# The sums of squares of one RMS norm on ScalarE instead of VectorE's statistics, in a four-layer kernel on one core

## The reference

```python
def _rmsnorm(x, w):
    n = xf * jax.lax.rsqrt(jnp.mean(xf * xf, axis=-1, keepdims=True) + EPS)
    return n.astype(x.dtype) * w
...
h = x + _gqa(_rmsnorm(x, attn_norm_w), wq, wk, wv, wo)
out = h + _moe(_rmsnorm(h, ffn_norm_w), gate_w, expert_w)
```

## Time and profile before

| what | value |
|---|---|
| three timed runs | 1502.51, 1512.09, 1514.85 us; median 1512.09 |
| the profiled execution | 1492.19 us, span of its instructions 1490.4 us |
| mean granted clock of TensorE | 0.902 |
| TensorE busy | 1239.1 us, 83% |
| VectorE busy | 1028.9 us, 69% |
| ScalarE busy | 838.9 us, 56% |
| GpSimd busy | 773.5 us, 52% |

### The profile page before, as it was taken

One profiled execution on the slowest core, in us unless ns is written; L12 is line 12 of the kernel. 1 busy time (PEld: TensorE's weight loads), 2 busy tenths in 40 slices (PEclk: granted clock), 3 DMA queues, 4 the chain that ended last, 5 costly groups with the idle time before them and its releaser, 6 DMA issues.

```text
span 1490.4 us, 39703 instructions
## 1 busy us (share of the span) xinstructions
PE 1239.1 (83%) x15796; PEld 959.4 (64%) x15797; DVE 1028.9 (69%) x2439; ACT 838.9 (56%) x2675; POOL 773.5 (52%) x793
## 2 busy tenths in 40 slices
PE   5878879878978888887898888778887578998997
PEld 4667667664756666666677656666665156776776
DVE  4467787886877687868568789886653856655562
ACT  3697676546459558657837645563543455434431
POOL 4048497486287419631762783781101767545442
PEclk8697888998989899999789899998998589999999
DMA  6000000000000000000000000001001000000000
GB/s 165 5 2 1 1 2 1 2 2 1 22 1 2 21 2 1 2 23 1 1 21 2 2 1 2 17 10 47 1 12 48 20 2 3 10 10 9 16 10 15
DMA packets 26703, 19.20 MB, mean 13 GB/s; under 512 B 6521, under 2 KB 24217, under 8 KB 26393
## 3 DMA queue, kind: packets, MB, share of 16 engines
q1 hardware_dynamic: 24936, 15.78, 3.7%
q10 hardware_dynamic: 1584, 0.89, 0.2%
HBM read 12.73 MB, written 3.93 MB: 11 GB/s over the span
## 4 chain that ended last, share of the span: by engine, by line
PE 25%; DVE 11%; ACT 6%; POOL 4%; issue 4%; POOLq 0%; ACTq 0%; DVEq 0%
PE bank L1164 4%; ACT arena L1219 2%; PE pair L1138 2%; DVE arena L1631 2%; PE bank L1207 2%; PE bank L1197 2%; PE bank L525 1%; PE bank L878 1%; PE pair L1111 1%; PE pair L495 1%; PE bank L530 1%; PE pair L853 1%; PE pair L826 1%; ACT arena L1266 1%; DVE arena L1635 1%
## 5 line engine op out<-in xcount | busy, mean ns | idle before, releaser
L1219 ACT ACTIVATE arena<-bank 128x512 f32<-128x512 f32 (+5 forms) x363 | 187.0, 545 | 253.9 <-PE bank L530 83.2
L1631 DVE TENSOR_REDUCE arena<-pair 128x8 f32<-128x1024 f32 (+2 forms) x224 | 240.3, 1095 | 101.2 <-PE pair L580 41.5
L2317 POOL TENSOR_TENSOR arena<-arena 128x512 f32<-128x512 f32 x160 | 184.6, 1153 | 65.7 <-DVE arena L1751 58.9
L1266 ACT ACTIVATE arena<-pair,arena 77x128 f32<-77x128 f32 x512 | 178.1, 369 | 27.4 <-DVE arena L1631 20.2
L2322 POOL TENSOR_TENSOR arena<-arena 128x512 f32<-128x512 f32 x128 | 182.5, 1426 | 10.0
L2255 POOL TENSOR_SCALAR arena<-arena 128x4 f32<-128x4 f32 x64 | 20.3, 317 | 266.4 <-DVE arena L1638 213.1
L2338 POOL TENSOR_TENSOR arena<-arena 128x512 f32<-128x512 f32 x64 | 67.2, 1065 | 147.4 <-ACT arena L1219 110.1
L525 PE MATMUL bank<-ident 128*128 128x128 f32 x780 | 126.5, 303 | 10.9 <-POOL subscale L2208 4.3
L525 PEld LDWEIGHTS bank<-ident 128*128 128x128 f32 x780 | 110.6, 211 | 29.3 <-issue 12.4
L2262 POOL TENSOR_SCALAR_AFFINE_SELECT arena<-arena 77x1024 f32<-77x1024 f32 x64 | 69.3, 1095 | 108.6 <-ACT arena L1603 108.2
L1603 ACT ACTIVATE arena<-pair 77x1024 f32<-77x1024 f32 x64 | 63.1, 1016 | 103.3 <-PE pair L1138 95.9
(11 more groups left out here) (304 smaller groups left out, 2990.3 us busy)
## 6 DMA issues: line engine op xcount, KB each, us to landing
arena<-in_ctx_turned SPq DMA_DIRECT2D x16, 154.0 KB, 2.6
arena<-in_x SPq DMA_DIRECT2D x8, 256.0 KB, 4.3
out<-arena SPq DMA_DIRECT2D x8, 256.0 KB, 2.5
spill<-arena SPq DMA_DIRECT2D x7, 256.0 KB, 2.0
arena<-spill SPq DMA_DIRECT2D x7, 256.0 KB, 5.1
arena<-in_ctx SPq DMA_DIRECT2D x8, 154.0 KB
arena<-in_ctx_turned SPq DMA_DIRECT2D x1, 1232.0 KB, 7.0
wexp<-in_L_ffn_expert_w SPq DMA_DIRECT2D x1, 512.0 KB, 4.2
```

The costliest lines, as they stand in the source:

```text
L1219: return act.activation(dst, src, func, bias=bias, scale=scale)
L1266: ins = act.activation(e0[0:CTX, (2 * SEQS * g + u) % 3, tokens(i)], o.bank[0:CTX, tokens(i)], ACT.Exp, bias=negmax0[0:CTX, u, i:i + 1], a ...
L1631: return dve.tensor_reduce(dst, src, X, op, **kw)
L2317: pool.tensor_tensor(into, xvs[:, b, ex * SHD:(ex + 1) * SHD].unsqueeze(1).broadcast_to([128, SH, SHD]), gates[g % 2][:, b, 0:SH, ex].unsq ...
```

## The change

The statistics of h and the two small products leave VectorE. ScalarE gets a new step at the start of its `m1`: four activations with the function Square, each over one sequence's 128 channels, whose accumulator gives the sum of squares. Their elementwise output goes to `nm`, which GpSimd overwrites later. The division by 128 is put into GpSimd's `rsqrt`. ScalarE's order string gets eight letters n, one a group; the other engines' strings and the fillers stay. The new step stands, in ScalarE's order, right behind: the copy of `ysT` of group 2 (group 0), of layer 1's `nT1` of group 2 (group 1), the second copy `eF` of a sequence of group 4 (group 2), layer 1's `aT1` of group 4 (group 3), the copy of `ysT` of group 6 (group 4), layer 2's last copy of group 4 (group 5), `aT1` of group 7 (group 6) and layer 2's last copy of group 6 (group 7).

```diff
@@ ORDER["A", "scalar"]: eight letters n added, the rest of the string is the same
@@ ScalarE
             def m1(g):
                 yield
+                o = E["f1", g, "o"]
+                act.wait_ge(o.drained, o.n + 1)
+                if g:
+                    act.wait_ge(m_x, g)
+                    act.wait_ge(lnm.n, g)
+                for b in range(SEQS):
+                    ins = act.activation(nm[:, b, :], hres[g % 2][:, b, :], ACT.Square, accum_out=lnm.mv[:, b, 1:2])
+                ins.then_inc(C.give(lnm.var), 1)
+                yield
                 o = E["m", g, "n"]
@@ VectorE
                 o = E["f1", g, "o"]
                 dve.wait_ge(o.drained, o.n + 1)
-                stats(lnm, h).then_inc(C.give(dve_step), 1)
-                dve.wait_ge(dve_step, C.last(dve_step))
-                tt(msq, lnm.mv[:, :, 0], lnm.mv[:, :, 0], ALU.mult).then_inc(C.give(dve_step), 1)
-                dve.wait_ge(dve_step, C.last(dve_step))
-                tt(lnm.mv[:, :, 1], lnm.mv[:, :, 1], msq, ALU.add).then_inc(C.give(lnm.var), 1)
                 tt(x, x, h, ALU.add)
@@ GpSimd
-            def rsqrt(dst, src, eps):
-                pool.tensor_scalar(dst, src, eps, None, ALU.add).then_inc(C.give(pool_step), 1)
+            def rsqrt(dst, src, eps, each=1.0):
+                if each == 1.0:
+                    pool.tensor_scalar(dst, src, eps, None, ALU.add).then_inc(C.give(pool_step), 1)
+                else:
+                    pool.tensor_scalar(dst, src, each, eps, ALU.mult, ALU.add).then_inc(C.give(pool_step), 1)
...
-            def spread(ln, eps):
+            def spread(ln, eps, each=1.0):
                 pool.wait_ge(ln.var, C.next(ln.var))
-                return rsqrt(ln.rstd, ln.mv[:, :, 1], eps)
+                return rsqrt(ln.rstd, ln.mv[:, :, 1], eps, each)
...
-                spread(lnm, RMS_EPS).then_inc(C.give(pool_step), 1)
+                spread(lnm, RMS_EPS, 1.0 / CH).then_inc(C.give(pool_step), 1)
```

More of the change, by code:

```diff
@@ L56 @@
         "wawwwaiabwbwwwwwwwbbbbbbcccaacabdbddbddebebdcfecfebfbfecefbfaaegfceafhffbbgfbbcfhbdcbgdddbdceheaabde"
[L57 to L62, removed]
+        "fgecffeafehfbfbgibfeecihfbgifbifcibffhibjcgjbdjjhcdglldddhedellfleleffiififleelgefifiehnfgfnfnfjnfjn"
+        "njhjnngnndnhdnldldnnllnglldnhnilldeeaeainefanibffbignennneinnihfbfnfnjcjbgjnjnbeechfnbfnfbgncfbnifhn"
+        "fcaagladldhddlldililbleelifeedibfiefnfecnbfnfjejnfegjnfnjfbnhnfgcbnnnfnfhbbgnllnchnbgcnillnhalaldail"
+        "liddiddbeibinebcnffdenjjfnebjnbncfejnnbefnfnbgnnefecffnbhnfcngnfnfillhadagaldlbdhddbebgebdchefcellff"
+        "bibibfiefegcefibfhecillfgjjffjjhnfdfngnldlndndndnnhdelelnnngnllnfenellnfefffhfnigennnnefeifnfinhninn"
+        "gififnnfhnngjnjjnjnhngllinhlliilylyilyyyyylyyyiyinyyynyjjynjjnnnnnllnnnllnnllnnllnnnnnnnnnnnnnnnnnnn",
     ("B", "scalar"):
```

## The result

The changed kernel is slower: the ratio to the kernel before on record is 1.0097, 95% interval 1.0067 to 1.0126, which is 14.6 us, where 8 were forecast. That ratio leaves out the executions of the kernel before that were more than 1.5% above its fastest, 9 of 20, and none of the changed kernel's, so it lies high. Over all 20 and 20 executions the medians are 1502.76 and 1512.87 us, 10.1 us apart, and the means 1502.9 and 1511.1 us: 8.2 us or 0.54%, 95% interval 3.5 to 12.9 us. A second measurement gave a ratio of 1.0106 (1.0065 to 1.0147), and 7.5 us between the means.

The account below looks back on a forecast made before the run. It named no single bound: in stage A four hand-ordered engines make each other late. Lateness of 9.7 us less VectorE's 1.68 gave +8.0 us on 1512.09, so 1520 us; 8 in 10 for 1502 to 1532.

Parts of the forecast that it names:

- small loss: Whole kernel: late norm in groups 1 to 6 outweighs VectorE's gain, +8 us, 1514 to 1526 us; chance 0.50.
- What is removed: VectorE, second norm's statistics: 1.68 us a group goes, 13.4 us in eight groups.
- What is added: ScalarE: four Square and accumulator-read pairs a group, 1.45 us, bounds 1.2 and 2.4; 11.6 us in all.
- lower bound that L1298's row gave: ScalarE's squares: by a 336 ns SBUF-to-SBUF activation a pair may cost some 0.30 us, 1.2 us for four.
- When the squares start: ScalarE's fixed order: never waits for `hres` but comes late, so normalised activations come 14.5 us later together.
- What is late next: Waits behind the squares and norm on TensorE, VectorE and GpSimd, group by group: 9.7 us of lateness paid.
- The sum: Stage A: 9.7 us of lateness less VectorE's 1.68 us credited once in group 0, leaving +8.0 us.
- VectorE as the bound: Stage A: VectorE's 13.4 us come off and ScalarE's lateness is absorbed, 1499 us; chance 0.11.
- Table loads: ScalarE: Square needs two table loads a group, 16 x 1.28 = 20.5 us, giving 1541 us; chance 0.05.
- Absorbed both ways: TensorE's idle stretches and fillers take it up; lateness and gain cancel, 1512 us; chance 0.22.
- All of GpSimd's lateness: Every wait for the norm counts: 14.5 us instead of 9.7, no VectorE gain, 1527 us; chance 0.12.
- Against which time: Base of the forecast: 8 us put on the 1512.09 us median of three timed runs, giving 1520 us.

Follow-up runs that it names:

- run without statistics: Kernel before with VectorE's statistics and two products removed and nothing in their place, GpSimd's root made of a constant; ratio 0.9989.
- relay without statistics: Kernel before, VectorE's statistics removed; GpSimd waits for a small ScalarE copy of a constant mean square at the change's place; ratio 1.0006.

## Why the prediction was right, and by how much it was off

It forecast a small loss from lateness in groups 1 to 6, and a small loss from lateness it is. The size came out near, 8.2 us between the means for 8.0, but in part by luck: the terms of the sum came to some 3 us less than forecast, and a part of the loss goes with TensorE's clock, which the sum had no term for. By its steps:

- *What is removed.* The block is gone and worth 13.4 us of VectorE time, as the sum had it. That the time hardly gains by it was right too (0.9989).
- *What is added.* 1.27 to 1.29 us for four pairs, not 1.45; the value lay near the lower bound that L1298's row gave. The squares take 302 ns on average, where the exponentials' first took 370. GpSimd's two-operation instruction stands at 0.19 us everywhere, where the addition took 0.5 to 0.6 beside VectorE.
- *When the squares start.* Right in all eight groups: ScalarE never waited for `hres`, and each block begins where the activation ahead ends. The root came later, against the end of `hres`, by 2.2, 2.6, 1.9, 0.9, 3.5, 1.2 and -0.4 us in groups 1 to 7, where 2.55, 2.83, 2.88, 1.17, 3.71, 1.51 and -0.16 were forecast: 11.9 us for 14.5. The shorter square is 1.2 us of the difference, and 0.7 more lies in group 3, where the second profile of the change has 2.6 us. The root and the scaling got 0.4 us shorter besides, so the norm's end is 9.1 us late in all.
- *What is late next.* Every wait named is in the trace, group 1's for ScalarE (0.83 to 1.06 us), group 3's for ScalarE (1.94 to 3.10), group 2's and 5's for GpSimd. How much later each place named comes against `hres`, as the mean of two profiles before and two after, groups 1 to 6: 0.8, 2.2, 1.2, -0.1, 3.1 and 0.3 us, where the sum had 1.45, 2.83, 1.45, 0.5, 2.7 and 0.9. In group 2 two profiles of one kernel differ by some 1.5 us. In group 5 VectorE's copy of the gate came 12.65 us after `hres` instead of 9.52. In group 7 the norm is 0.8 us sooner, where 0.16 was forecast.
- *The sum.* With these sizes it gives 6.7 us instead of 9.7, and 5.0 with VectorE's 1.68 set off once. At equal clock the change costs 4.1 and 5.3 us: so far the adding was sound. The rest, up to 8.2 and 7.5 us, goes with a mean clock of 0.886 and 0.890, where the kernel before had 0.892. The trace shows a way to it, half clock behind the new waits; how much of the rest is that and how much is the scatter of the clock isn't shown. Against the ratio's 14.6 us the sum is short by nearly half.
- *The rivals.* VectorE as the bound is ruled out by the run without statistics. Table loads: three, as before. Absorbed both ways is what the run with earlier squares shows, not the change. All of GpSimd's lateness (1527 us and more) isn't reached.
- *Against which time.* The median of three, 1512.09, was high: with 20 runs it is 1502.76. So the predicted 1520 us is 7 above the 1512.87 found: 9.3 us too much in the time before, and 2.1 too little in the change. The time found even lies in the stretch given to *absorbed both ways* (1507 to 1514) and not in that of the small loss (1514 to 1526); it is the comparison with the kernel before that shows the loss. The range of 1502 to 1532 holds the time in either case.

What stays open is how far lateness itself brings the clock down. The kernels with a late norm and VectorE's block in place have the lowest mean clock (0.884, twice) and those in which the squares are in time the highest (0.896, 0.898), which speaks for it. The kernel with the squares done twice speaks against a plain rule: its norm is the latest and its mean clock is 0.890, as in the change's second series. Single profiles can't decide it: both profiles of before are of short executions, those without statistics and of the relay without statistics (1514.20 us) are of long ones, and the part before the first changed instruction alone shifts by up to 12 us.

## What to carry to other kernels

When work moves to another engine with a fixed order, compare two clocks for each repetition: when its input is ready, and when the engine's queue comes to it. Moving the squares one to four steps up in ScalarE's order took 1.1% down to 0.2% by the ratios, 9.2 us over all executions, with no other edit; the sizes of the two blocks (1.27 us against 1.68) didn't decide it. Time saved on an engine that isn't late is worth little, here 13.4 us of VectorE for 0.1%. And where the executions of one kernel spread by 2%, an effect of 0.5% is read from the means over all of them, with the granted clock beside, and not from two profiles.

## What the runs showed of the hardware that was not expected

GpSimd's root and scaling on the same data took 2.41 us in the change, from 577.57 to 579.98, and 2.75 us before: L2255 0.53 us then and 0.19 now. Before, VectorE's addition of x (L1926) ran beside it; so it did in each of the seven groups in which L2255 took 0.52 to 0.60 us, and in group 0, without it, L2255 took 0.22. The instructions behind the one of 577.57 shown above, same timeline:

```profile
577.84 1.02 POOL L2264 TENSOR_TENSOR arena<-arena,minushalf 128x4 f32<-128x4 f32 x1
578.94 1.04 POOL L2274 TENSOR_TENSOR arena<-arena 128x512 f32<-128x512 f32 x1
```

The time from the start to `hres` of group 0 was 315 to 329 us in fourteen profiles, though up to there no instruction's order differs but for one or two initial ones in the kernels without statistics. It goes with the granted clock of TensorE in that stretch: 0.85 at 317 us, 0.82 at 324, 0.80 at 325 and 329. The 35 timed executions of the kernel before in one series reach from 1479 to 1515 us, with a mean clock from 0.909 to 0.878.
